# Plain columns' matmuls with both halves of the weights side by side, and VectorE adding the two parts

## What is computed

```python
def layer0(x, c, weight, c_weight, bias, W, b, A, B, gate_w, gate_b):
    y = grouped_conv1d(x, weight, taps=9, groups=4) + (c @ c_weight.T)[:, :, None] + bias[None, :, None]
    out = y @ W.T + b                                    # 1024 x 1024
    probs = softmax(y @ gate_w.T + gate_b)               # 4 ranks, the best one is taken, weight p / p
    return x + out + (y @ A[:r].T @ B[:, :r].T)          # r of 8, 16, 32, 64 by the gate

def layer1(x, e, W0, b0, W1, b1, W2, b2, weight, bias_k, W_base, b_base, W_router, b_router, A, B):
    att = softmax(mlp(e))                                # 8 kernels mixed for each sample
    y = mix(att, weight) @ x + (att @ bias_k)[:, :, None]
    out = y @ W_base.T + b_base
    w = sparsemax(y @ W_router.T + b_router)             # 8 experts
    return x + out + sum_e(w[e] * (y @ A[e]) @ B[e])     # rank 16 each
```

## Time and profile before

| | us |
|---|---|
| median of 3 runs | 510.87 (510.73 to 511.74) |
| profiled execution, run | 512.81 |
| profiled execution, span | 511.0 |

### The profile page before, as it was taken

How to read it: one execution, slowest core, us unless ns; L and a number is a source line. 1 busy time by engine, 2 the same in 40 slices (tenths; PEclk the granted TensorE clock), 3 DMA queues, 4 the chain that set the end, 5 groups by cost and what they waited for, 6 DMA issues and landing times.

```text
span 511.0 us, 8700 instructions
## 1 busy us (share of the span) xinstructions
PE 504.3 (99%) x3221; PEld 477.7 (93%) x3221; DVE 350.2 (69%) x768; ACT 131.4 (26%) x272; POOL 140.8 (28%) x122
## 2 busy tenths in 40 slices
PE   9999999999999999999999999999999999999997
PEld 8999999999999999999989998999999999999986
DVE  3956988748676666765888766665738667585852
ACT  4732334222233113231342321210212121111200
POOL 1000010012443340433105262431506244170620
PEclk9999999999999999999999999999999999999999
DMA  8845204439466755638899652433424233430212
GB/s 315 312 150 162 83 1 147 153 105 278 140 209 210 248 192 207 192 126 300 262 408 368 228 179 70 146 98 123 128 71 165 74 127 102 132 138 19 103 45 83
DMA packets 41126, 84.36 MB, mean 165 GB/s; under 512 B 3803, under 2 KB 24667, under 8 KB 41084
## 3 DMA queue, kind: packets, MB, share of 16 engines
q1 hardware_dynamic: 31884, 61.16, 35.6%
q10 hardware_dynamic: 9200, 22.65, 12.3%
HBM read 58.82 MB, written 24.97 MB: 164 GB/s over the span
## 4 chain that ended last, share of the span: by engine, by line
PE 90%; DMA 4%; DVE 2%; issue 1%; POOL 1%; ACT 1%; ACTq 0%; DVEq 0%; POOLq 0%
PE b_x L1248 6%; PE b_x L1250 6%; PE b_x L1251 6%; PE b_m L1197 5%; PE b_p L1231 5%; PE b_p L1230 5%; PE b_p L1232 5%; PE b_y L1248 4%; PE b_y L1251 4%; PE b_y L1250 4%; PE b_m L1207 3%; PE b_z L1250 2%; PE b_y L1197 2%; PE b_z L1251 2%; PE b_z L1248 2%; DMA wb_raw<-in_wcat 2%
## 5 line engine op out<-in xcount | busy, mean ns | idle before, releaser
L556 ACT CAST a_hi<-mixed 128x512 fp32r<-128x512 f32 x63 | 38.1, 620 | 166.4 <-DVE mixed L858 88.5
L870 DVE TENSOR_TENSOR s_lo<-mixed,s_hi 128x512 fp32r<-128x512 f32 x56 | 63.6, 1156 | 18.0 <-ACT s_hi L568 16.1
L504 POOL TENSOR_TENSOR xs<-xs,mixw_sb 128x464 f32<-128x464 f32 (+1 forms) x28 | 38.2, 1376 | 119.1 <-DMA xs<-x_scratch 119.1
L1231 PE MATMUL b_p<-wp_lo,a_hi 128*128 128x232 f32 (+1 forms) x224 | 61.7, 275 | 0.0
L1230 PE MATMUL b_p<-wp_hi,a_hi 128*128 128x232 f32 (+1 forms) x224 | 61.4, 274 | 0.0
L1232 PE MATMUL b_p<-wp_hi,a_lo 128*128 128x232 f32 (+1 forms) x224 | 61.3, 274 | 0.0
L568 ACT CAST s_hi<-mixed 128x512 fp32r<-128x512 f32 x56 | 34.8, 622 | 76.6 <-POOL mixed L476 37.1
L863 DVE TENSOR_TENSOR a_lo<-mixed,a_hi 128x512 fp32r<-128x512 f32 x63 | 46.0, 755 | 11.3 <-ACT a_hi L556 10.7
L952 DVE TENSOR_TENSOR xs<-b_x,xs 128x464 f32<-128x464 f32 (+1 forms) x54 | 33.5, 621 | 29.2 <-PE b_x L1251 24.8
L476 POOL TENSOR_TENSOR mixed<-mixed 128x512 f32<-128x512 f32 x13 | 16.8, 1292 | 120.4 <-DVE a_lo L863 120.4
L1231 PEld LDWEIGHTS b_p<-wp_lo,a_hi 128*128 128x128 f32 x224 | 42.9, 192 | 0.2
(11 more groups left out here) (258 smaller groups left out, 1241.7 us busy)
## 6 DMA issues: line engine op xcount, KB each, us to landing
blk<-x_scratch SPq DMA_DIRECT2D x16, 512.0 KB, 3.3
blk<-in_xblk SPq DMA_DIRECT2D x14, 516.0 KB, 4.0
xs<-in_x SPq DMA_DIRECT2D x16, 296.0 KB, 4.6
x_scratch<-xs SPq DMA_DIRECT2D x16, 296.0 KB, 3.6
w_raw<-in_wcat SPq DMA_DIRECT2D x8, 546.0 KB, 8.2
xs<-x_scratch SPq DMA_DIRECT2D x14, 280.0 KB, 3.4
out_dram<-xs SPq DMA_DIRECT2D x14, 280.0 KB, 2.5
praw<-in_wcat ACTq DMA_DIRECT2D x8, 464.0 KB, 4.7
```

Of the source, the lines that this page charges most:

```text
L504: pool.tensor_tensor(x_rows, x_rows, bbase[:, a:b], ALU.add).then_inc(x_biased[q], 1)
L556: act.copy(a_hi[:, op, :, :], mixed[:, op, :, :]).then_inc(ahi_done[op], 1)
L870: dve.tensor_tensor(s_lo[:, i, :, :], mixed[:, S_AT[i], :, :], hi(s_hi[:, i, :, :]), ALU.subtract).then_inc(slo_done[i], 1)
L1231: pe.matmul(dst, x_hi, wp_lo[:, k, 0:PLAIN[l]], start=False, stop=False)
```

## The change

The high and low halves of the plain weights come to lie side by side, in one tensor `wp` with a middle index of 2, and so do those of the rank weights (`lb`). In `plain`, x_hi is multiplied with both halves in one matmul, whose two outputs (2 x 228 or 2 x 232 columns) lie side by side in the same PSUM bank (`wide`); x_lo by w_hi is added to the first. The two outputs are then added by VectorE: the gate's columns with a reduction ahead of the gate into a new tile `hid_sb` (`hidden`), the output columns in `take_plain` with two additions onto the rows of x in place of one. In layer 1 the rank part of the plain columns does the same (`lora_rest`). Pairs 0 and 1 are as before. Further: GpSimd waits for both gates of a pair ahead of `add_base(3, g)` in pairs 9 to 15; in pair 7, VectorE splits the first tile's transposed gate result ahead of a `sum_mix`, and the two halves of the B11 split move behind `sum_mix` and behind the take of P6; the load of `bk` has no semaphore of its own any more and is waited for with `pk`.

```diff
@@ -112,17 +112,18 @@
...
         with (nc.sbuf_tensor("wb_raw", [P, SLOTS, HK, HMAX], F32) as wb_raw,
-              nc.sbuf_tensor("wp_raw", [P, NCH, PMAX], F32) as wp_raw,
-              nc.sbuf_tensor("lb_raw", [P, D], F32) as lb_raw):
+              nc.sbuf_tensor("wp_place", [P, NCH, 2, PMAX], F32) as wp_place,
+              nc.sbuf_tensor("lb_place", [P, 2, D], F32) as lb_place):
             pass
         wb_lo = sb("wb_lo", [P, SLOTS, HK, HMAX], F32R)
-        wp_lo = sb("wp_lo", [P, NCH, PMAX], F32R)
-        lb_lo = sb("lb_lo", [P, D], F32R)
+        wp = sb("wp", [P, NCH, 2, PMAX], F32R)
+        lb = sb("lb", [P, 2, D], F32R)
+        wp_hi, wp_lo, wp_raw = wp[:, :, 0, :], wp[:, :, 1, :], wp_place[:, :, 1, :]
+        lb_hi, lb_lo, lb_raw = lb[:, 0, :], lb[:, 1, :], lb_place[:, 1, :]
         with nc.sbuf_tensor("wb_rows", [P, SLOTS, HK, HMAX], F32) as wb_rows:
...
         wb_hi = sb("wb_hi", [P, SLOTS, HK, HMAX], F32R)
-        wp_hi = sb("wp_hi", [P, NCH, PMAX], F32R)
-        lb_hi = sb("lb_hi", [P, D], F32R)
         a_hi = sb("a_hi", [P, 4, HK, P], F32R)
@@ -160,6 +161,7 @@
...
         gs = sb("gs", [P, 4, EXP])
+        hid_sb = sb("hid_sb", [P, HID1])
@@ -184,7 +186,7 @@
...
         s_taps = [sem("s_taps0"), sem("s_taps1")]
-        s_front, s_mlp, s_bk, s_mixw = sem("s_front"), sem("s_mlp"), sem("s_bk"), sem("s_mixw")
+        s_front, s_mlp, s_mixw = sem("s_front"), sem("s_mlp"), sem("s_mixw")
         s_lb, s_bias0, s_bbase = sem("s_lb"), sem("s_bias0"), sem("s_bbase")
@@ -225,6 +227,7 @@
...
         gated, ut_done = sem("gated"), sem("ut_done")
+        rest_half, hid_done = sem("rest_half"), sem("hid_done")
@@ -278,6 +281,11 @@
...
             return part[:, D // 2 * n:D // 2 * (n + 1)]
+        def wide(s):
+            return b_p[s][:, 0:2 * PMAX].rearrange("p (v c) -> p v c", v=2)
@@ -517,6 +525,8 @@
...
                     add_base(2, g)
+                    if g > PAIRS:
+                        pool.wait_ge(gated, 4 * (2 * g + 2))
                     add_base(3, g)
@@ -652,7 +662,7 @@
...
             act.dma_start(blk[0][:, 0:GROUPS * QX], xblk[0][:, 0:GROUPS * QX]).then_inc(s_sample[0], 16)
-            act.dma_start(bk[:, :], bias_k).then_inc(s_bk, 16)
+            act.dma_start(bk[:, :], bias_k).then_inc(s_mlp, 16)
             split_w(0)
@@ -880,6 +890,20 @@
...
+            def hidden(T):
+                l = layer(T // 2)
+                both = wide(T % 2)[:, :, REST[l]:PLAIN[l]]
+                dve.wait_ge(pl_done, T + 1)
+                if T < 2 * FULL:
+                    return both[:, 0, :]
+                if T > 2 * FULL:
+                    dve.wait_ge(gated, 4 * T)
+                total = hid_sb[:, 0:PLAIN[l] - REST[l]]
+                dve.tensor_reduce(total, both.rearrange("p v c -> p c v"), AX_X, ALU.add).then_inc(hid_done, 1)
+                dve.wait_ge(hid_done, T - 2 * FULL + 1)
+                return total
             def gate0(T):
@@ -889,8 +913,7 @@
...
                 s = T % 2
-                hid = b_p[s][:, REST[0]:PLAIN[0]]
-                dve.wait_ge(pl_done, T + 1)
+                hid = hidden(T)
                 if T > 1:
@@ -919,8 +942,7 @@
...
                 s = T % 2
-                hid = b_p[s][:, REST[1]:PLAIN[1]]
-                dve.wait_ge(pl_done, T + 1)
+                hid = hidden(T)
                 dve.wait_ge(ut_done, T - 1)
@@ -960,7 +982,11 @@
...
                 x_rows = rows_at(g)[s][:, 2 * HALF[l]:D]
-                dve.tensor_tensor(x_rows, b_p[s][:, 0:REST[l]], x_rows, ALU.add).then_inc(finq[s], 1)
+                parts = wide(s)[:, :, 0:REST[l]]
+                if g >= FULL:
+                    dve.tensor_tensor(x_rows, parts[:, 1, :], x_rows, ALU.add).then_inc(rest_half, 1)
+                    dve.wait_ge(rest_half, 2 * (g - FULL) + s + 1)
+                dve.tensor_tensor(x_rows, parts[:, 0, :], x_rows, ALU.add).then_inc(finq[s], 1)
@@ -1116,9 +1142,12 @@
...
                     take_first(g)
+                if g == PAIRS - 1:
+                    split_ut(2 * g)
                 if g < LAST:
                     sum_mix(2 * g + 2, 0)
-                split_ut(2 * g)
+                if g != PAIRS - 1:
+                    split_ut(2 * g)
                 if g < LAST:
@@ -1143,14 +1172,14 @@
...
                 take_plain(0, g)
-                if g == PAIRS - 1:
-                    split_slot(B11, 0)
                 if g < LAST and g != PAIRS:
...
                 if g == PAIRS - 1:
-                    split_slot(B11, 1)
+                    split_slot(B11, 0)
                 dve.wait_ge(p_done[P6], made(g))
                 take(b_x, 1, g, took_u2)
+                if g == PAIRS - 1:
+                    split_slot(B11, 1)
                 if g == PAIRS:
@@ -1221,15 +1250,16 @@
...
                 pe.wait_ge(finq[s], g)
-                dst = b_p[s][:, 0:PLAIN[l]]
+                both = wide(s)[:, :, 0:PLAIN[l]]
+                dst = both[:, 0, :]
                 for k in range(NCH):
...
                     x_hi, x_lo = a_hi[:, op, k % HK, :], a_lo[:, op, k % HK, :]
-                    pe.matmul(dst, x_hi, wp_hi[:, k, 0:PLAIN[l]], start=(k == 0), stop=False)
-                    pe.matmul(dst, x_hi, wp_lo[:, k, 0:PLAIN[l]], start=False, stop=False)
-                    ins = pe.matmul(dst, x_lo, wp_hi[:, k, 0:PLAIN[l]], start=False, stop=(k == NCH - 1))
+                    pe.matmul(both, x_hi, wp[:, k, :, 0:PLAIN[l]], start=(k == 0), stop=False, skip_group_check=True)
+                    ins = pe.matmul(dst, x_lo, wp_hi[:, k, 0:PLAIN[l]], start=False, stop=(k == NCH - 1),
+                                    skip_group_check=True)
                 ins.then_inc(pl_done, 1)
@@ -1282,6 +1312,18 @@
...
                 ins.then_inc(done, 1)
+            def lora_rest(T, done):
+                s, h = T % 2, HALF[layer(T // 2)]
+                if T < TILES:
+                    lora(T, b_p[s], 2 * h, D, done)
+                else:
+                    both = wide(s)[:, :, 0:D - 2 * h]
+                    pe.wait_ge(utlo_done, T + 1)
+                    pe.matmul(both, ut_hi[:, s, :], lb[:, :, 2 * h:D], start=False, stop=False, skip_group_check=True)
+                    pe.matmul(both[:, 0, :], ut_lo[:, s, :], lb_hi[:, 2 * h:D], start=False, stop=True,
+                              skip_group_check=True).then_inc(done, 1)
@@ -1345,7 +1387,7 @@
...
                 if step == 0:
-                    pe.wait_ge(s_mlp, 16)
+                    pe.wait_ge(s_mlp, 32)
                     mlp(0, first_in[:, FR_C:FR_C + NB])
@@ -1380,7 +1422,6 @@
...
                     if g == 0 and k == 6:
-                        pe.wait_ge(s_bk, 16)
                         pe.wait_ge(att_copied, 1)
@@ -1484,7 +1525,7 @@
...
                 lora(t1, b_z, 0, h, c11_done)
-                lora(t1, b_p[0], 2 * h, D, q_done[0])
+                lora_rest(t1, q_done[0])
                 if g < LAST:
@@ -1495,7 +1536,7 @@
...
                 lora(t2, b_w, 0, h, c21_done)
-                lora(t2, b_p[1], 2 * h, D, q_done[1])
+                lora_rest(t2, q_done[1])
                 if g == AGG_PAIR:
...
                     aggregate(1)
```

## The result

| | before | after |
|---|---|---|
| median of 22 runs each, us | 511.90 | 509.19 |
| profiled execution, run | 512.81 | 509.43 |
| profiled execution, span | 511.0 | 507.7 |

After is faster: the ratio of the times is 0.9946, 95% interval 0.9936 to 0.9956, so 2.3 to 3.3 us are saved. The three runs of before that the prediction stood on had a median of 510.87; 22 have one of 511.90.

The account below looks back on a forecast made before the run. TensorE was taken as the bound, with a floor of some 111 ns per matmul. Terms +0.4 - 1.0 + 0.4 + 0.1 - 1.2 - 2.4 = -3.7 us, from 510.87, gave 507.1 us; range 504.7 to 509.5.

Parts of the forecast that it names:

- (b): Change of layer swallows pairs 3 to 6's gain, keeps a gap: 509.1 us; or two-piece wide matmuls cost more: 509.3 to 510.9; chance 0.15.
- (d): Plain tiles: a wide matmul costs what its two halves cost, 223 ns, so 2.4 us are missing: 509.5 us; chance 0.04.
- Floor and wide matmul: Plain tiles: each matmul costs at least some 111 ns; wide ones take 207 (layer 0) or 210.8 ns (layer 1).
- Rank part: Layer 1 plain columns: three matmuls of 96 become 192 and 96, saving one floor, 0.11 us a tile, 1.8 us in all.
- Reductions: VectorE ahead of each gate: 0.3 us in layer 0, 0.43 in layer 1; with the additions, 19 us more on VectorE.
- Pairs 3 to 6: Layer 0's ordinary pairs: 2.3 us of slack holds the added VectorE work, so 4 x 0.26 = 1.0 us is gained.
- Pair 2: Two reductions delay the split, turn_u comes at 97.35: the pair loses 0.4 us instead of gaining 0.26.
- Change of layer: Pairs 7 and 8: the 0.99 us gap goes, pair 8's turn_u comes 0.4 us later, rank part nets 0.1 us more.
- Pair 9: The GpSimd wait removes 0.74 us of TensorE idle time; with 0.20 and 0.22 us from merged matmuls, 1.2 us gained.
- Pairs 10 to 15: Layer 1's ordinary pairs: 6 x (0.20 + 0.22) = 2.5 us gained, less 0.1 in the last pair.
- (c): VectorE paces every pair at the second turn_u, with reductions from 1.0 us on: slower, about 516 us; chance 0.07.
- (a): No stalls come: reductions at 0.25 us and the change of layer keeps its gain: 504.7 us; chance 0.16.

Follow-up runs that it names:

- e6: Before, with the plain matmul of x_hi by w_lo cut to its first 128 of 228 or 232 columns; 511.85 us, ratio 1.0001 to before.
- e2: After, with layer 1's plain-column rank part as three matmuls of 96 columns again; 511.07 us, ratio 0.9976 to before.
- e5: After, with every reduction ahead of a gate made twice; 511.70 us, ratio 0.9993 to before.
- e4: After's layout and orders, but narrow plain and rank matmuls, no reduction and no second addition; 512.47 us, ratio 1.0008 to before.
- e11: The e8 kernel with hid_sb placed behind all other tiles, a 2 KB spare tile ahead of it; 507.25 us, ratio 0.9889 to before.
- e15: Before, with only an unused 544-byte tile where the change puts hid_sb; 513.12 us, ratio 1.0016 to before.
- e8: After, with pair 2's split ahead of the first sum_mix and pair 8's later GpSimd additions waiting for rank-weight splits; 507.25 us, ratio 0.9907 to before.
- e13: Before, unchanged, profiled a second time to see how its gaps vary; 512.61 us in its one run.
- e1: After, without GpSimd's wait for both gates in pairs 9 to 15; 511.74 us, ratio 0.9979 to before.
- e3: Before, with only the GpSimd wait and pair 7's moved splits, narrow matmuls, no reduction; 512.28 us, ratio 0.9999 to before.
- e14: The e3 kernel run once more, unchanged, against before; 511.06 us, ratio 0.9979.

## Why the prediction came out as it did

The sign and the mechanism were right, and 509.19 us lies in the range, near its upper end: 2.1 us above the 507.1, a little outside the forecast's own 505.3 to 509, and where rival (b) had put its first case (509.1). The total alone would not tell the forecast from that rival or from (d), at 509.5; the rows do. Of these, 1.0 us is the base: I set the difference on 510.87, the median of three runs, and 22 runs have 511.90. The other 1.0 us is the difference itself, -2.7 by the medians instead of -3.7. That the two profiles came as near as -3.4 is partly luck: pairs 2 to 8 came 0.9 us worse than forecast, pairs 9 to 15 0.4 better, and the gap of pair 9 was larger in the profile of before than in the three other traces of that code. Point by point:

- **Floor and wide matmul.** Right: 207 and 211 ns, 0.27 us a pair in layer 0 in the plain tiles themselves. e6 shows the same floor for 128 columns as for 228 and 232. By the formula for an isolated matmul in the page "TensorE: Matmul & The Clock Gate" of the Trainium skill, section "Back-to-back issue gap", two matmuls of 232 columns merged into one would have saved 2.5 ns (the prediction has 2.6); the traces show 12.6. The same section says that this formula under-counts at few columns, and gives 81 ns at 128 columns and 131 at 512 for a stream of weight loads and matmuls, which the prediction passed over; the traces deny these too, with 111 ns at 128 columns and already 211 at 464.
- **Rank part.** Right: 0.25 us a pair in e2 for a forecast of 0.22.
- **Reductions.** They were right in size (0.29 and 0.44 us), and the slack of ordinary pairs was there (e5). The 19 us more on VectorE left out what the wait on GpSimd takes from the gates.
- **Pairs 3 to 6.** Forecast -1.0, came -0.78. The step that failed is "the layout ... cost nothing: TensorE has other work there". The plain matmuls gained the 0.27 us, and 0.08 us a pair went in the products with S, because `hid_sb` moved s_hi by 544 bytes (e4, e11, e15).
- **Pair 2.** Forecast +0.4, came +0.74. The mechanism was right, the term was 0.3 us too small: turn_u came at 97.46 where I had 97.35 (its split came 0.71 us later than before, not 0.6), the matmul after an idle turn_u started 0.13 us behind it and not 0.03, and 0.08 us went to the layout. e8 shows the remedy: the order of pair 7, in pair 2.
- **Change of layer.** The second turn_u of pair 7 stayed where it was (252.77 against 252.70), and the 0.99 us before the seventh product went, both as forecast. The first turn_u of pair 8 was forecast at 278.8 and came at 278.05, before the old 278.40: the chain through the weight loads was not later. But that place varies between executions (e13), and the same code gave 277.46 in e1. The rank part of pair 8 waited 0.95 us and not 0.35. The step that failed is "run longer into VectorE's splits: 0.35 us more": I counted the added time on the `lb` split alone, and the two a_lo ahead of it, which took 3.36 us instead of 1.28 without GpSimd, were what grew. Also, my sum was not well kept there: 278.8 was a place against before, and I added its +0.4 on top of the -0.6 that pairs 2 to 6 had brought by then. With places throughout, the sum would have been +0.4 + 0.1 - 1.2 - 2.4 = -3.1.
- **Pair 9.** Forecast -1.2, came -1.39. The trace agrees, and the price of the interference is real (e1: 1.7 us by the ratios in the changed kernel). But the 0.74 us of the earlier trace rows was what one execution had: in the four traces pair 9 was 0.93, 0.35, 0.02 and 0.01 us above its shortest, 0.33 on average. The profiled execution of before was, at 512.81 us, 0.9 us above its median, that of after 0.2 above its own; that is the 0.7 us by which the profiles' difference (3.4) exceeds the medians' (2.7).
- **Pairs 10 to 15.** Forecast -2.4, came -2.6. e1 shows that this hangs on the wait: without it these pairs together are only 0.2 us shorter than before. I had given the wait no value from pair 10 on.
- **Rivals.** (c) is false (e5). (d) is false by the rows of the wide matmuls. (a) would have needed no idle time in pairs 2, 7 and 8; with most of it gone, e8 gains 2.0 us and comes near (a)'s size: 1 - 0.9907 is 4.8 us of 512.30, without a slower change of layer. Of (b), the first half was partly so: gaps at the change of layer went and others came, at +0.81 us for pairs 7 and 8.
- **GpSimd against VectorE.** The page "SBUF — State Buffer" of the Trainium skill, section "Who interferes with whom", says that a VectorE instruction with two SBUF inputs contends with a GpSimd instruction that reads SBUF. The traces agree: 3.36 against 1.28 us for the same two operations (e8).

Three things stay open: what the orders and the wait are worth without the wide matmuls (e3 and e14: 0 to 1 us); why the address of S counts; and what sets the floor of 111 ns, since in every run each matmul has a weight load of its own.

## What to carry to other kernels

Where narrow matmuls are all spaced alike whatever their columns, put two that share their stationary operand side by side in one PSUM bank, and let an engine with slack add the parts: two floors give way to the price of the columns, here 13 to 16 ns less for a merged matmul and 0.11 us less for a rank part, so count them before you begin. The gain is kept only if the chain behind the added operation has slack in every stage: look stage by stage at the first waits that end late, and move splits ahead of sums and another engine's SBUF additions behind the critical chain, as e1 and e8 show for 1.7 and 2.0 us, where the whole change gained 2.7. And read two or three traces before a single gap goes into a sum: one that hangs on a transfer comes and goes.

## What was unexpected in the hardware

- An address in SBUF has a price here: 544 bytes more ahead of s_hi make a pair of layer 0 0.07 to 0.10 us longer (31.19 to 31.28 us in the kernel before, 30.94 to 31.01 in the mended one), spread thinly, mostly over the products with S, at 432 columns; in layer 1 it was 0.02 or 0.03 us in the kernel before and 0.01 or less in the mended one.
- GpSimd's additions on SBUF stretch VectorE's operations with two SBUF inputs, and are themselves stretched: 3.36 us instead of 1.28 for two subtractions, 0.69 instead of 0.17 for 8 columns, 2.20 instead of 1.39 for an addition.
- What a transfer releases moves by about 1 us between executions of kernels with the same code at that place, in pair 9 (6.8 to 8.2 us into the pair) and at the change of layer (26.8 to 27.65 us from the start of pair 6), and in the traces TensorE's time moves with it.
- A matmul whose columns lie in two pieces, with a gap of 4 or none in PSUM, costs what one in a single piece costs: 464 columns 211 ns (210.8 in one piece), 456 columns 207 ns, on the line between 432 and 464.
